# Softmax attention on one core: the weighted sums of two super-steps in one run of sixteen matmuls, with a longer ring of probabilities

## The reference

```python
q = _qdq(x) @ _qdq(wq).T + bq               # int8-like rounding of rows
k, v = split(cond @ wkv.T + bkv)            # 2 batches, 1024 keys each, 16 heads of 32
attn = softmax(einsum('bnhd,bmhd->bhnm', q, k) / sqrt(32))
o = einsum('bhnm,bmhd->bnhd', attn, v)
out = _qdq(o) @ _qdq(wp).T + bp
```

## Time and profile before

| what | value |
|---|---|
| median of 3 runs | 1945.07 us (1944.83 to 1945.47) |
| profiled execution, its own time | 1949.54 us |
| its span | 1947.8 us |
| mean granted TensorE clock | 0.979 of full |
| TensorE (PE) busy | 1845.8 us, 95% of the span |
| VectorE (DVE) busy | 1275.5 us, 65% |
| ScalarE (ACT) busy | 701.8 us, 36% |
| GpSimd (POOL) busy | 403.4 us, 21% |

### The profile page before, as it was taken

How to read it: one execution, slowest core, us unless ns; L and a number is a source line. 1 busy time by engine, 2 the same in 40 slices (tenths; PEclk the granted TensorE clock), 3 DMA queues, 4 the chain that set the end, 5 groups by cost and what they waited for, 6 DMA issues and landing times. The chain is left out here.

```text
span 1947.8 us, 24670 instructions
## 1 busy us (share of the span) xinstructions
PE 1845.8 (95%) x9304; PEld 1384.6 (71%) x9304; DVE 1275.5 (65%) x2133; ACT 701.8 (36%) x1123; POOL 403.4 (21%) x306
## 2 busy tenths in 40 slices
PE   7999999899999999989999999999989999799998
PEld 5777886444443568758888888888878875678887
DVE  5334755665761666676787787687763398866766
ACT  3302232344445468733342342342334331212211
POOL 0000100211200258720121121111200011443532
PEclk9999998999999899999999999999999999899999
DMA  5102222232321311133122222313212100101101
GB/s 217 44 0 70 87 71 51 54 74 69 81 68 29 102 66 65 44 115 97 64 92 76 93 88 100 97 60 117 92 35 76 65 23 22 60 28 44 44 1 43
DMA packets 90374, 132.57 MB, mean 68 GB/s; under 512 B 11264, under 2 KB 54272, under 8 KB 88720
## 3 DMA queue, kind: packets, MB, share of 16 engines
q1 hardware_dynamic: 90256, 131.00, 21.4%
HBM read 97.21 MB, written 14.75 MB: 57 GB/s over the span
## 5 line engine op out<-in xcount | busy, mean ns | idle before, releaser
L802 DVE TENSOR_REDUCE b_nm<-ps 128x1 f32<-128x1024 f32 x128 | 153.1, 1219 | 91.1 <-PE ps L790 91.1
L1288 ACT ACTIVATE b_pr<-ps 128x512 f32<-128x512 f32 x256 | 133.5, 603 | 135.4 <-PE ps L1200 135.2
L248 PE MATMUL ps<-d_x_high,d_w_high 128*128 128x512 f32 x384 | 154.6, 403 | 1.7 <-issue 1.7
L249 PE MATMUL ps<-d_x_low,d_w_high 128*128 128x512 f32 x384 | 149.9, 390 | 0.0
L250 PE MATMUL ps<-d_x_high,d_w_low 128*128 128x512 f32 x384 | 149.9, 390 | 0.0
L2249 POOL TENSOR_TENSOR d_sqsum<-d_sqsum,d_sq 128x512 f32<-128x512 f32 x32 | 46.1, 1445 | 467.8 <-ACT d_sq L2161 467.5
L1212 PE MATMUL ps<-b_pr,b_VS 128*64 128x512 f32 x512 | 131.2, 636 | 0.0
L1745 POOL TENSOR_TENSOR c_h<-c_h,c_w_row 128x512 f32<-128x512 f32 x64 | 105.7, 1657 | 50.5 <-DMA c_w_row<-w_rows 27.8
L1200 PEld LDWEIGHTS ps<-b_qS,b_kS 98*128 98x128 f32 x256 | 44.1, 193 | 78.5 <-issue 52.3
L1200 PE MATMUL ps<-b_qS,b_kS 98*128 98x512 f32 x256 | 93.2, 447 | 6.9 <-ACT b_pr L1288 3.5
L790 PE MATMUL ps<-b_kS,b_qS 96*128 96x512 f32 x256 | 82.7, 408 | 5.9 <-DVE b_nm L802 4.5
(11 more groups left out here) (441 smaller groups left out, 5027.8 us busy)
## 6 DMA issues: line engine op xcount, KB each, us to landing
b_kS<-b_k_parts SPq DMA_DIRECT2D x96, 128.0 KB, 2.3
f_rows<-d_fw SPq DMA_DIRECT2D x24, 512.0 KB, 2.8
f_w<-f_rows SPq DMA_DIRECT2D x12, 1024.0 KB, 4.8
c_w_row<-w_rows SPq DMA_DIRECT2D x16, 512.0 KB, 3.5
b_qS<-b_q_parts SPq DMA_DIRECT2D x96, 64.0 KB, 2.0
a_convT<-in_convT SPq DMA_DIRECT2D x4, 1024.0 KB, 13.1
d_w<-in_d_wq SPq DMA_DIRECT2D x16, 256.0 KB, 2.8
d_w<-in_d_wk SPq DMA_DIRECT2D x16, 256.0 KB, 3.0
```

Source lines behind the costliest of these rows:

```text
L248: nc.tensor.matmul(out, lhsT[0], rhs[0], start=start, stop=False)
L249: nc.tensor.matmul(out, lhsT[0], rhs[1], start=False, stop=False)
L802: nc.vector.tensor_reduce(nm[:, g % 2, u:u + 1], c.ps[:, banks:banks + 2, :], AX.XY, ALU.max, negate=True).then_inc(job_read, 1)
L1288: nc.scalar.activation(pr[:, n % RING, :], c.ps[:, 4 + n % BANKS, :], ACT.Exp).then_inc(exp_done, 1)
```

## The change

The `weigh` calls of two super-steps are issued together, in every second super-step: after the scores and jobs of an even `ss`, those of `ss`-2 and `ss`-1, which are eight fp32 matmuls or sixteen records. An odd super-step has no `weigh`. The ring grows from 8 to 12 slots. Slots 8 to 11 lie at 52 and 60 KB while n < PR_LATE = 176, and from there on at 68 KB, where keys that are already split lie. Because the slots at 52 to 68 KB are where `load_shared` writes, SyncE now waits before it until 88 `weigh` calls are done (`PR_LATE // 2`). ScalarE waits once, before tile 176, that group 6 has been split.

```diff
+    pr_early = [c.at(f"b_pr_early{i}", [P, 2, BANK], F32, kb) for i, kb in enumerate((52, 60))]
+    pr_late = c.at("b_pr_late", [P, 4, BANK], F32, 68)
...
-    RING, BANKS = 8, 3
+    RING, BANKS = 12, 3
+    PR_LATE = 11 * 4 * KT // 2
...
+    def prob(n):
+        slot = n % RING
+        if slot < 8:
+            return pr[:, slot, :]
+        return pr_early[slot % 8 // 2][:, slot % 2, :] if n < PR_LATE else pr_late[:, slot - 8, :]
...
                 if g == 5:
+                    sp.wait_ge(av_done, PR_LATE // 2)
                     head.load_shared(sp)
...
-                                            VS[:, 2 * (q % 2) + hh, k * VW:k * VW + VPAD], pr[:, (n + hh) % RING, :],
+                                            VS[:, 2 * (q % 2) + hh, k * VW:k * VW + VPAD], prob(n + hh),
...
-                if ss >= 1:
-                    weigh(4 * (ss - 1))
-                    weigh(4 * (ss - 1) + 2)
+                if ss >= 2 and ss % 2 == 0:
+                    for n in range(4 * (ss - 2), 4 * ss, 2):
+                        weigh(n)
...
-                nc.scalar.activation(pr[:, n % RING, :], c.ps[:, 4 + n % BANKS, :], ACT.Exp).then_inc(exp_done, 1)
+                if n == PR_LATE:
+                    act.wait_ge(split_done, 2 + 4 * 6)
+                nc.scalar.activation(prob(n), c.ps[:, 4 + n % BANKS, :], ACT.Exp).then_inc(exp_done, 1)
```

## The result

The changed kernel takes 1967.57 us (median of 4 runs, 1967.12 to 1970.17) against 1944.95 us (4 runs, 1944.15 to 1945.47): a ratio of 1.0122, 95% interval 1.0109 to 1.0134, 22.6 us slower. Forecast were 1965 us, 1953 to 1976, slower with 0.82.

A forecast was written before the change was run, and what follows sets the result against it. TensorE's stream was taken to set the pace in stretches full of maxima; 6.3 (rounds) + 9.5 (stall) + 1.7 + 2.5 (clock) = +20.0 us on 1949.5, 1969.5, or 1965 at the median, range 1953 to 1976.

The forecast's parts named there:

- Switches: TensorE entering and leaving runs of weighted sums: 31 fewer at 0.34 us, 10.5 us saved at most.
- The wait for VectorE in plain double rounds: Fourth max job (D) waits for the second's reduce, cancelling the saved switch: 7.89 us against 7.88, 0 in all.
- A step after job A: Five double rounds with a VectorE step after the first max job: about +0.6 us each, +3.3 in all.
- Where VectorE is the limit: Six double rounds where jobs outnumber slots, with the maxima wait at super-step 8: +4 us, between 0 and +7.
- Pair and turn rounds: Six double rounds with a pair or turn among the jobs: -0.1 to -0.3 us each, -1 in all.
- No maxima: Super-steps 53 to 62, ScalarE decides: +0.17 us, or -0.3 where a result is moved; about 0 over five.
- The stall: Super-step 45's first job waits for stack(7, 0), queued behind load_shared on SyncE: +9.5 us, between 8.8 and 12.7.
- The clock: TensorE at half clock: +1.7 us after the wait at super-step 45, +2.5 where VectorE limits.
- The base: The sum was added to the profiled execution, 1949.5 us, then lowered to 1965 because that execution stood 4.5 above the median.
- the one with saved switches: Rival, chance 0.12: switches saved in full, VectorE doesn't hold the fourth max job; +0.7 us, 1946.
- the ones without a stall: Rivals at super-step 45: no stall, switches saved, 1935 us (0.06); stall hidden, VectorE holds as said, 1954 (0.08).
- the one with many falls of the clock: Rival, chance 0.12: six or more further stretches at half clock, +10 us on the sum, 1975.

The follow-up runs named there:

- x6: As x1, but VectorE reduces only one of each max job's two banks, so maxima cover half the keys; 1925.15 us, ratio 0.9909 to the kernel before.
- x1: Changed kernel with load_shared and its wait moved from g = 5 to g = 6, behind the last stack(7, h); 1953.08 us, ratio 1.0053.
- x2: Kernel before the change with only the wait for 88 weigh calls added ahead of load_shared; 1962.17 us, ratio 1.0093.
- x8: Changed kernel with late load_shared and a table choosing single, double or last-job-behind-the-run order for each pair of super-steps; 1945.78 us, ratio 1.0001.
- x7: Changed kernel with the wait left in g = 5 and the seven loads alone moved to g = 6; 1961.32 us, ratio 1.0093.

## Why the prediction was right

- **Switches.** 0.34 us each and 31 of them, 10.5 us at most. The removal shows in the waits; that it is real money shows in x6, where 0.27 of a double round come through.
- **The wait for VectorE in plain double rounds.** Walked to 7.89 us, measured 7.90, with D's load at 3.65. Shown by the release in the trace and by x6.
- **A step after job A.** +0.6 each forecast; +0.6, +0.6, +0.6 and +0.5 at 15, 19, 35 and 49 (at 49, with two steps, the sum had 0.9). At 17, where a pair job comes in as well, +4.4: 0.5 by the walk, 0.9 from a bias step that GpSimd held up (last section), and 3.1 of clock, since x1 took 10.31 us there at full clock and the changed kernel 13.36. That clock loss was in my sum only as a lump.
- **Where VectorE is the limit.** +4 forecast, +1.4 measured. 3/4, the clean case, took +0.07 where I had +0.3. 5/6 took 2.6 us less than before, and that is luck: x2 and x8 have single rounds there too and took 14.09, as the changed kernel did (14.03). In the kernel before the clock fell there, for 6.9 us. The other seven of this group come to +4.0, the figure of the forecast, with 3.4 us more at half clock than before near super-step 38.
- **Pair and turn rounds.** -0.08 and -0.26 measured where -0.1 and -0.2 stood; 13/14 got 1.9 us back because the clock did not fall there. It did not in x2 either, whose rounds are those of the kernel before (10.27 us), so 1.6 of the 1.9 are not the change's doing.
- **No maxima.** +0.2 and -0.25 in turn, as walked. At 55/56 a wait for the maxima rows added 0.5, which I had not named.
- **The stall.** The mechanism was right, the size low: 9.5 taken, 12.2 measured, within the bounds of 8.8 to 12.7. The mis-sized term is the loads' data ahead of the copies, for which I took 0.7 and the bound gave 3.9; it is 3.4. The rule that descriptors start in order within one queue of one DMA engine (the Trainium skill, "DMA: Bandwidth & Descriptors", section "Two DMAs through the same engine are not ordered") stood beside that bound. The landing times agree with it: 5.4 and 4.7 us behind the loads, 2.3 and 2.0 without them.
- **The clock.** x1 took 10.2 us for 45/46 at full clock. The 26.3 us less 12.2 of stall and these 10.2 leave 3.9 for the clock, against 1.7 for the 3.4 us at half clock in that place before: +2.2 where I had +1.7. Elsewhere I had +2.5. What came is a loss of 3.1 at 17/18 and 3.4 us more at half clock near super-step 38, against gains at 13/14 (1.6) and 5/6 (2.6), where the clock had fallen before.
- **The base.** The sum, +20.0, was put on a profiled execution that lay 4.5 us above its median. The loop in the profiles grew by 19.6, the span by 17.8 (1947.8 to 1965.6) and the medians by 22.6. The 2.6 us between 1965 and 1967.6 can't be given to a term: the profiled execution before was 4.6 us longer than its median, the one after 0.2 shorter, and where the median runs before saved those 4.6 us no trace shows.
- **How much of the number was luck.** The sum hit the loop's growth within half a microsecond (20.0 forecast, 19.6 measured), but its terms did not. The steps after A and 45/46 came 3.4 and 3.05 us above their forecasts; the VectorE group, the pair and turn rounds and the lump for the clock came 2.6, 1.7 and 2.5 below. The stall and the cost of double rounds are shown by experiment; that the misses cancelled is chance.

Of the rivals, the one with saved switches falls by x1 and the double round's 7.90; the ones without a stall by the 12.04 us wait; the one with many falls of the clock by the trace, which has four stretches at half clock in the loop, where the one before has five. They last 47.8 us together against 27.3, and 17 us of the difference are in and behind the stall.

## What to carry to other kernels

A wait on an in-order DMA queue is paid by whatever stands behind it: move it behind every transfer that is due soon, and count the issue time and the data of what is released with it. Merging runs to save a switch also merges what the runs kept apart; walk one merged round to the job that holds it before counting the switches, since an engine that is idle for a third of the round can be its limit. And what a round saves in a loop of dependent stages can be taken back at the next wait with a fixed time, here the rows of the maxima. A pair of super-steps is worth comparing only with several traces of the same order: single falls of the clock were worth 1.6 to 3 us, as much as most of the effects looked for.

## What the hardware showed that I had not expected

**A VectorE step and GpSimd.** The walk gave 9.4 us for 17/18. x1, where the clock stays at full speed there, took 10.31. The missing 0.9 is in the bias step. In the changed kernel it starts 0.04 us after a cast of GpSimd and takes 1.54 us instead of 0.68: 0.86 longer, where the cast lasts 1.04. First VectorE, then GpSimd:

```profile
415.90 1.54 DVE L1399 TENSOR_TENSOR x<-x,b_bp 128x512 f32<-128x512 f32 x1
```

```profile
415.86 1.04 POOL L835 CAST b_k_parts<-b_KF 128x1024 fp32r<-128x1024 f32 x1 [1.45 <-DMA b_qS<-b_q_parts]
```

The Trainium skill, page "SBUF — State Buffer", section "Who interferes with whom", says that a VectorE operation with two inputs in SBUF and a GpSimd operation that reads SBUF take a shared pair of ports in turn, and the later one waits for the whole of the other. The traces agree with it. In the kernel before, the same bias step begins 0.58 us ahead of the same cast and takes 0.68; the next one begins inside another GpSimd instruction and takes 1.33:

```profile
420.20 0.68 DVE L1387 TENSOR_TENSOR x<-x,b_bp 128x512 f32<-128x512 f32 x1
420.78 1.04 POOL L826 CAST b_k_parts<-b_KF 128x1024 fp32r<-128x1024 f32 x1 [2.06 <-DMA b_qS<-b_q_parts]
424.68 1.28 POOL L829 TENSOR_TENSOR b_q_parts<-b_qF,b_q_parts 128x512 fp32r<-128x512 f32 x1
425.18 1.33 DVE L1387 TENSOR_TENSOR x<-x,b_bp 128x512 f32<-128x512 f32 x1
```

The ten traces hold 80 such bias steps. In 67 no GpSimd instruction was under way at the start, and all took 0.68 us. In 13 one was, and each of these ended 0.54 to 0.55 us after that instruction's end, however early or late it had begun. So the delay follows the GpSimd instruction. No kernel here moved the cast on purpose, but its place differs among the traces, and the step's length goes with it.

**The clock can't be placed.** Super-steps 17 and 18 took 13.36 us in the changed kernel, 11.87 in x7 and 10.31 in x1, and the streams of the three agree to far beyond that point. In the changed kernel TensorE paused 1.46 us for VectorE, and the granted clock was 0.50 for the 6.8 us after it:

```profile
416.90:418.30 1.40, 0.27 (x2) 0.00 (x0) 1.40 (x2) 1.08 (x2) 1.40 (x2) 1.00 0.00 0
418.30:421.70 3.40, 3.07 (x8) 2.03 (x10) 2.63 (x5) 1.09 (x2) 3.16 (x2) 0.50 0.02 5
421.70:425.10 3.40, 3.40 (x10) 0.94 (x10) 1.45 (x2) 0.00 (x0) 0.00 (x0) 0.50 0.00 0
```

In x1 the same instructions stand 3.0 us later, TensorE paused as long, and the clock stayed at 1.00:

```profile
419.90:421.30 1.40, 0.28 (x2) 0.00 (x0) 1.40 (x2) 1.08 (x2) 1.40 (x3) 1.00 0.02 6
421.30:424.70 3.40, 3.04 (x14) 1.63 (x16) 3.10 (x5) 1.09 (x2) 3.21 (x2) 1.00 0.02 5
```

A term for the clock can be bounded by such rows, but not tied to a place.
